# A graph network on one core: the masked features made three table steps ahead, and the first layer's rows stored ahead of its dense blocks

## The reference, cut to what matters

```python
# graph attention: k, q, v by node type, then a 16x16 matrix per head and edge type
k = _typed_linear(x, Wk, ntype).reshape(N, H, D)
q = _typed_linear(x, Wq, ntype).reshape(N, H, D)
v = _typed_linear(x, Wv, ntype).reshape(N, H, D)
kw = _typed_rel(k[src], rel_att, etype)
a = (kw * q[dst]).sum(-1) * rel_pri.T[etype] / sqrt(D)
m = _typed_rel(v[src], rel_msg, etype)
...
# three times, after the attention and a layer norm
h = x @ W
agg = segment_sum(h[src] * norm[:, None], dst)
agg = agg + b
```

## Time and profile before

| What | Value |
|---|---|
| median of 3 executions | 4404.68 us (4403.91 to 4405.47) |
| the profiled execution's own time | 4402.57 us |
| its span, first to last instruction | 4400.2 us |
| mean granted TensorE clock | 0.888 of full speed |
| table stage, by the trace | to about 594 us |
| attention stage | about 594 to 1950 us |
| normalizations, last scatters | about 1950 to 2165 us |
| three graph layers | about 2165 to 4370 us |

### The profile page before, as it was taken

How to read it: one execution, slowest core, us unless ns; L and a number is a source line. 1 busy time by engine, 2 the same in 40 slices (tenths; PEclk the granted TensorE clock), 3 DMA queues, 4 the chain that set the end, 5 groups by cost and what they waited for, 6 DMA issues and landing times.

```text
span 4400.2 us, 57750 instructions
## 1 busy us (share of the span) xinstructions
PE 3591.3 (82%) x17006; PEld 2515.2 (57%) x17006; DVE 2413.3 (55%) x8286; ACT 1140.0 (26%) x2513; POOL 2612.3 (59%) x2737
## 2 busy tenths in 40 slices
PE   3677758888888777665499999979999969999993
PEld 3565557778777666662355555545555545555552
DVE  3334447777777656569245444445544454554446
ACT  1111147887778565542200000000000000000001
POOL 0000047666667777778577777737677755767772
PEclk8788878898888777878799999989999979999996
DMA  6787867777783333320387888758788858778871
GB/s 189 226 292 291 291 229 280 280 284 270 270 289 99 87 94 91 88 79 1 108 334 292 299 300 300 285 193 299 286 298 299 300 187 301 293 289 299 299 290 49
DMA packets 273376, 1026.64 MB, mean 233 GB/s; under 512 B 66086, under 2 KB 126021, under 8 KB 234160
## 3 DMA queue, kind: packets, MB, share of 16 engines
q1 hardware_dynamic: 157760, 714.07, 43.6%
q0 software_dynamic: 103792, 266.94, 18.4%
q10 hardware_dynamic: 11520, 41.95, 3.3%
HBM read 797.16 MB, written 225.58 MB: 232 GB/s over the span
## 4 chain that ended last, share of the span: by engine, by line
PE 62%; POOL 17%; DVE 9%; issue 7%; DMA 2%; SPq 2%; ACT 0%; POOLq 0%; DVEq 0%; ACTq 0%
PE bank L1003 36%; POOL arena L518 8%; PE bank L975 8%; POOL a_tab L498 7%; PE bank L843 3%; PE bank L858 3%; PE bank L861 3%; PE bank L792 2%; DVE arena L1052 2%; PE bank L803 2%; PE bank L789 2%; POOL stage L543 1%; PE bank L778 1%; PE bank L1008 1%; DVE arena L1150 1%
## 5 line engine op out<-in xcount | busy, mean ns | idle before, releaser
L543 POOL DMA_INDIRECT stage<-h_tab,earr x1536 | 1453.0, 946 | 715.8 <-issue 362.1
L1003 PE MATMUL bank<-arena,xr 128*128 128x512 f32 (+1 forms) x3822 | 1695.0, 590 | 44.5 <-DMA arena<-a_tab 38.6
L1003 PEld LDWEIGHTS bank<-arena,xr 128*128 128x128 f32 x3822 | 698.4, 191 | 758.7 <-issue 742.4
L518 POOL DMA_INDIRECT arena<-kv_tab,idxr x832 | 801.0, 963 | 351.6 <-issue 241.8
L1508 DVE TENSOR_TENSOR sums<-sums,bank 128x128 f32 x1536 | 432.9, 282 | 815.4 <-PE bank L975 809.2
L1479 DVE TENSOR_SCALAR oh<-iota_j,earr 128x128 f32<-128x128 f32 x1536 | 585.4, 384 | 87.7 <-DVE sums L1499 45.3
L698 ACT ACTIVATE rs<-mv,epsc 128x49 f32<-128x49 f32 (+1 forms) x6 | 1.9, 316 | 2114.5 <-DVE mv L1542 2012.8
L975 PEld LDWEIGHTS bank<-oh,stage 128*128 128x128 f32 x3072 | 409.0, 196 | 233.8 <-issue 187.8
L843 PE MATMUL bank<-xr,arena 128*128 x3328 | 435.2, 290 | 77.3 <-DVE arena L1204 50.3
L975 PE MATMUL bank<-oh,stage 128*128 128x128 f32 x3072 | 420.8, 282 | 51.1 <-DMA stage<-h_tab,earr 41.6
L843 PEld LDWEIGHTS bank<-xr,arena 128*128 128x128 f32 x3328 | 414.9, 205 | 82.2 <-issue 81.0
(11 more groups left out here) (216 smaller groups left out, 3065.2 us busy)
## 6 DMA issues: line engine op xcount, KB each, us to landing
arena<-a_tab SPq DMA_DIRECT2D x273, 1792.0 KB
a_tab<-stage SPq DMA_DIRECT2D x60, 1792.0 KB
a_tab<-sums POOLq DMA_DIRECT2D x31, 1792.0 KB, 11.9
kv_tab<-stage SPq DMA_DIRECT2D x48, 768.0 KB, 8.2
arena<-rel_d SPq DMA_DIRECT2D x52, 512.0 KB, 15.4
stage<-h_tab,earr POOLq DMA_INDIRECT x1536
arena<-key_d ACTq DMA_DIRECT2D x40, 512.0 KB, 5.0
arena<-in_edge_weight ACTq DMA_DIRECT2D x40, 512.0 KB, 8.4
```

The lines of the kernel that those rows point to most:

```text
L518: G.indirect_dma_start(kv[b % 3][:, t, :], None, kv_tab, bass.IndirectOffsetOnAxis(idxr[:, b % 3, t:t + 1], 0))\
L543: G.indirect_dma_start(gring[:, (q % NG) * GRP + s, :], None, h_tab[l], bass.IndirectOffsetOnAxis(src_i[:, t:t + 1], 0)).then_inc(row_land ...
L1003: mm = M.matmul(o_[:, 0:cw], xr[:, n, :], abuf[B % NBUF][:, n % KB, 0:cw], start=n == 0, stop=n == NT - 1)
```

## The change

VectorE makes one more tile's masked copies ahead of the loop, and in step n makes those of tile n+3 in place of n+2, in the other of the two buffers. `mask_x(n+3)` waits for the transposes of tile n+1. The number of instructions is the same.

On SyncE the first layer no longer loads four blocks first. It stores the 13 chunks and signals `tab_complete`, then waits for the scatters, then loads all 91 blocks. The wait for `types_done` is gone. Layers two and three keep their order.

```diff
-            sp.wait_ge(cells_saved, 16 * T1)
-            sp.wait_ge(types_done, NT)
             for l in range(3):
-                for b in range(NBUF):
-                    a_block(l, b)
+                if l:
+                    for b in range(NBUF):
+                        a_block(l, b)
                 for c, (c0, cw) in enumerate(CH):
                     sp.wait_ge(hrow_ready, NCH * l + c + 1)
...
                 sp.wait_ge(rows_saved, 16 * NCH * (l + 1))
                 sp.sem_inc(tab_complete, 1)
-                for b in range(NBUF, NBLK):
+                if l == 0:
+                    sp.wait_ge(cells_saved, 16 * T1)
+                for b in range(NBUF if l else 0, NBLK):
                     a_block(l, b)
...
             mask_x(0, 0)
             mask_x(1, 1)
+            mask_x(2, 0)
 
             def table(n, par):
-                if n + 2 < NT:
-                    mask_x(n + 2, par)
+                if n + 3 < NT:
+                    mask_x(n + 3, 1 - par)
                 copy_tab(n, n // 2, par)
```

## The result

The changed kernel takes 4266.66 us (median of 4 executions, 4264.99 to 4269.21) against 4404.3 us for the kernel before (four executions, where the table of the kernel before had three): a ratio of 0.969, 95% interval 0.967 to 0.970, or 137.6 us less. I had predicted 4312 us, in a range of 4282 to 4358. The direction was right; the size was not, and the range missed the result by 15 us.

What follows compares the result with a forecast made beforehand. A ring of waits between engines, not an engine, was taken to bound the table steps, with DMA next. Gains of 61 + 20 + 11 = 92 us from the profiled 4402.6 us, adjusted to the median, gave 4312 us, range 4282 to 4358.

Steps and rivals of the forecast that it cites:

- The ring: Table steps: mask, TensorE's transposes and products, copies and sums wait on each other in turn, setting 10.25 us a step.
- TensorE's order covers the mask's new wait: Table steps: the awaited transposes precede a product VectorE already waited for, so no cost; otherwise at most 2.70 us.
- The sign I had named: Table steps: transposes waiting for no mask would show the forecast right; they had idled 2.70 us.
- TensorE's own bound of 7.5 us a step: Table steps: TensorE's busy time, 271.51 us over 36 steps, as its limit once it no longer idles for the mask.
- So the stretch can't be shorter than 321 us: First sum to table's end: DMA share 0.79 of 406.5 us taken as 321 us of work that must be done.
- the range's low end: Steps with sums: largest gain 88 us, at share 1.01; with all terms' largest gains 4275 us, taken as 4282.
- Fullness 0.93: Steps with sums: DMA share assumed after the change, between 0.89 and 1.01, giving 345 us, a gain of 61 us.
- The limit of about 358 GB/s: Steps with sums: the skill's HBM figure for one core, 327 us for 117 MB; not held as a hard limit.
- First steps, 20 us: Table steps 0 to 8 and first keys: copies follow edge groups at once; gain 20 us, bounds 5 and 30.
- the 26: First table steps: 26 us gained from edge saves starting to land sooner, if landings stay as long.
- The first layer, 11 us: First layer: stores ahead of block loads remove TensorE's 9.25 us idle and the slow restart; gain 11 us.
- Rival C, landings: Table steps: landing of saves replaces the ring, costing time above 18.2 us; slower, 4417 us; chance 0.03.

Runs made afterwards that it cites:

- e4: Kernel before, with one zero write in the table stage instead of 31 and the other 90 at three per batch in the attention stage: 4460.84 us, ratio 1.012.
- e1: Changed kernel with only the masks made three steps ahead, SyncE's first-layer order as in the kernel before: 4283.55 us, ratio 0.972.
- e3: Changed kernel, with one zero write in the table stage instead of 31 and the other 90 at three per batch in the attention stage: 4254.72 us, ratio 0.965.
- e2: Changed kernel with only SyncE's first-layer order changed, masks two steps ahead as in the kernel before: 4397.81 us, ratio 0.998.
- e8: Changed kernel with 23 zero writes in the table stage instead of 31 and the first scatter at batch 36 instead of 32: 4258.61 us, ratio 0.967.
- e5: Changed kernel without 37 of the 40 pairs of key and weight loads, so part of the computation is left out: 4203.55 us, ratio 0.954.
- e9: Changed kernel with a third buffer for the table's tiles: 5440.37 us on a chip where the kernel before takes 5542.06 us.
- e11: Changed kernel with 17 zero writes in the table stage and a third table buffer: 5367.37 us on a chip where the kernel before takes 5542.06 us.

## Why the prediction was wrong in size

- **The ring sets the 10.25 us: right.** e4 takes 45 MB out of the steps and they stay; e1 gives the whole gain of the table.
- **TensorE's order covers the mask's new wait: right.** VectorE's masks wait for TensorE 1.8 us in the whole run. The sign I had named, transposes that wait for no mask, holds in the steps shown but not in all: 15 transposes still wait, 34.8 us in all, because VectorE comes late to the mask when its sums have waited for key loads.
- **TensorE's own bound of 7.5 us a step: wrong, though it changed nothing here.** It was the busy time at a clock of 0.83. The changed kernel needs about 7.3 us a step, and e3, at that bound, 5.6 us with a clock of 0.97.
- **"So the stretch can't be shorter than 321 us": wrong, and this is the step that failed.** It took 298.0, so that even the range's low end, a gain of 88 us from 318 us, was too small. I read the share of busy DMA engines as work, 0.79 x 406.5. For the saves that holds within 1 us across four kernels, and the zero writes took 104.5 and 103.4 us in the two that have them. For the key loads it does not: 155.0, 141.5, 136.4 and 106.7 us for 40.4 to 40.8 MB. In 3 us of the kernel before in which the key loads' queue was the only active one, the share was 0.93 at 217 GB/s; two more such windows (426 to 429 and 456 to 459 us) have 0.75 at 209 and 0.79 at 234. Just behind the first, with the two queues of writes active and almost no key load, it was 1.04 at 443 GB/s (windows, the last two columns):

```profile
313.50:316.50 3.00, 2.39 (x11) 2.39 (x12) 0.56 (x1) 0.60 (x1) 0.00 (x0) 0.60 0.93 217
317.50:322.00 4.50, 4.15 (x22) 2.74 (x20) 1.87 (x7) 0.87 (x3) 0.00 (x0) 1.00 1.04 443
```

  So an equal share stands for different amounts of data, and the earlier trace rows had shown it: 206 GB/s at 0.65 is 317 for a full share, 288 at 0.79 is 365, 403 at 1.01 is 399. Had I asked for GB/s at a full share, the floor would have been an estimated 117 MB at the 403 GB/s of the earlier trace rows, 290 us. At 0.96 of that rate, the fullness known only now, the gain would have been 104 us, against 108.5 measured.
- **Fullness 0.93: too low,** 0.96 measured. This is 11 us of the 47.5 missing (321/0.93 - 321/0.96); the other 36 are the floor.
- **The limit of about 358 GB/s** that the Trainium skill gives (DMA: Bandwidth & Descriptors, Specifications) is, by its own row, a stack's 716 GB/s divided by two cores, and would have put the stretch at no less than an estimated 327 us. The trace of this one core moved 390 GB/s over 298 us, so as a cap on it the figure doesn't hold here.
- **First steps, 20 us: right, 18.1 measured,** and by the mechanism. The landing behind copy 1 grew from 15.2 to 23.9 us (64.22 to 88.12), and behind copy 5 from 18.8 to 25.6 us; this took back some of the 26.
- **The first layer, 11 us: right, 11.0 measured,** and 9.7 us by e2's median.
- **Rival C, landings:** saves now land in up to 16.6 us (median 10.4), under the 18.2 from which it would cost. It didn't cost here, though the landing of saves is 32.3% of the chain that ended last; in e8 it sets the step while the pairs last.

## What to carry to other kernels

A chain through several engines in their written order can set a step although no compute engine is busy more than three quarters of it; issuing its head one step earlier took TensorE's waits for it from 104.3 to 34.8 us with one instruction moved ahead of the loop and none added. Before using a DMA share as a floor, divide GB/s by the share in several windows: if the result differs between them, the share is no measure of work, and the floor is better taken from the bytes at the best rate seen. When a stage has become bound by transfers, look for transfers in it that another stage could carry, and move only as many as that stage can take: 14 moved zero writes, kept at two per batch by starting the scatters later, gained 37 and 40 us over the changed kernel. 30 moved ones at three per batch gained 12 us (19 by the ratios, since e3's chip runs the kernel before 3 us slower), because the other stage gave back 74.

## What the runs showed of the hardware that I had not expected

- The engine time of the key loads (512 KB, one row of 4 KB read for each of 128 partitions) differs between runs with other transfers beside them: 155.0 us for 40.4 MB with only saves beside them and the engines at 0.57, 106.7 us for 40.7 MB with the engines at 0.96. The key loads' time doesn't follow the share alone: e8 has 118.8 us at 0.94. Writes of 1792 KB kept theirs per MB within 2%, and so did the saves of 768 KB in all runs but e5, where they took 78.9 us in place of 75.6. What in the engine makes the difference was not tried.
- A mixed stretch of loads and writes moved 390 GB/s for 298 us, and 412 GB/s over 50 us of it (200 to 250 us).
- One chip ran the kernel before in 5542 us. The three changed kernels profiled on it (e9 to e11) had a table stage of the usual length; in e9 the gathers of the attention stage spread over 2124 us (477.6 to 2601.9), 1.6 times the 1336 us of the changed kernel (472.1 to 1808.5).
